# A decoder block's opening rearranged: norm, query projection, copy jobs and the first q block on other engines and in another order

## The reference

```python
xn = (x - mu) * rsqrt(var + 1e-05) * ln_gamma + ln_beta
q = (xn @ Wq.T + bq); k = (xn @ Wk.T + bk); v = (xn @ Wv.T + bv)
p = (pos_emb @ Wpos.T)
content_score = einsum('bthd,bshd->bhts', q + u_bias, k)
pos_score = rel_shift(einsum('bthd,phd->bhtp', q + v_bias, p))
attn = softmax((content_score + pos_score) / sqrt(dh))
x = layernorm(x + einsum('bhts,bshd->bthd', attn, v) @ Wout.T + bout)
...                                   # cross attention, layernorm
x = layernorm(x + moe(x))             # the last norm writes the output
```

## Time and profile before

| | |
|---|---|
| time, median of 3 runs (range) | 167.94 us (167.81 to 168.45) |
| the profiled execution: time, span | 167.27 us, 165.5 us |
| busy: PE, DVE, ACT, POOL | 142.8 (86%), 114.3 (69%), 100.9 (61%), 99.7 (60%) us |
| mean granted TensorE clock | 0.954 |

### The profile page before, as it was taken

One profiled execution on the slowest core, in us unless ns is written; L12 is line 12 of the kernel. 1 busy time (PEld: TensorE's weight loads), 2 busy tenths in 40 slices (PEclk: granted clock), 3 DMA queues, 4 the chain that ended last, 5 costly groups with the idle time before them and its releaser, 6 DMA issues.

```text
span 165.5 us, 5090 instructions
## 1 busy us (share of the span) xinstructions
PE 142.8 (86%) x2069; PEld 106.7 (64%) x2073; DVE 114.3 (69%) x331; ACT 100.9 (61%) x204; POOL 99.7 (60%) x125
## 2 busy tenths in 40 slices
PE   6739987999899999879898999599999979999920
PEld 2114436777689999767646767467779766766810
DVE  5610953989999998998636679952992899865150
ACT  3685753499698987389982451646665515665112
POOL 7669993047387677558978610606895605955642
PEclk9975999999999999999999999879999999999995
DMA  4560023320024550000004100000000000000001
GB/s 154 159 260 0 0 49 82 84 49 4 6 67 98 155 118 6 4 0 4 6 0 118 60 4 0 0 0 0 2 4 0 0 0 6 32 32 0 0 0 63
DMA packets 5593, 6.72 MB, mean 41 GB/s; under 512 B 1051, under 2 KB 4739, under 8 KB 5443
## 3 DMA queue, kind: packets, MB, share of 16 engines
q1 hardware_dynamic: 4995, 5.88, 12.5%
q10 hardware_dynamic: 576, 0.53, 1.0%
HBM read 3.79 MB, written 0.52 MB: 26 GB/s over the span
## 4 chain that ended last, share of the span: by engine, by line
PE 51%; DVE 14%; ACT 13%; POOL 12%; issue 4%; DMA 3%; SPq 1%; ACTq 0%; POOLq 0%; DVEq 0%
PE ps L849 49%; POOL pl L433 4%; ACT moe_c L545 4%; POOL rstd L392 3%; ACT ph L549 3%; POOL off L396 2%; DMA x_sb<-in_x 2%; PE ps L949 2%; DVE pm L696 2%; ACT q_c L493 1%; DMA qd<-q_dn 1%; SPq L361 1%; POOL ve L389 1%; DVE xh L733 1%; DVE st L639 1%
## 5 line engine op out<-in xcount | busy, mean ns | idle before, releaser
L433 POOL TENSOR_TENSOR pl<-moe_c,ph 128x1024 f16<-128x1024 f32 x16 | 34.0, 2133 | 20.0 <-ACT ph L549 20.0
L442 POOL TENSOR_TENSOR ph<-ph 128x512 f32<-128x512 f32 x16 | 20.6, 1291 | 21.1 <-PE ps L849 10.4
L849 PE MATMUL ps<-qd,kp 128*128 128x32 f16 (+1 forms) x768 | 24.7, 193 | 1.9 <-DMA qd<-q_dn 1.3
L849 PEld LDWEIGHTS ps<-qd,kp 128*128 128x128 f16 x768 | 23.6, 98 | 4.2 <-ACT q_dn L519 1.8
L696 DVE TRANSPOSE_TENSOR_REDUCE pm<-ps 128x32 f32<-128x1024 f32 x16 | 20.0, 1249 | 5.0 <-PE ps L849 4.4
L849 PE MATMUL ps<-moe_c,ph 128*128 128x128 f32 x144 | 19.6, 282 | 0.2 <-POOL ph L442 0.2
L849 PEld LDWEIGHTS ps<-moe_c,ph 128*128 128x128 f32 x144 | 17.4, 191 | 2.7 <-issue 2.4
L545 ACT ACTIVATE moe_c<-ps 128x1024 f32<-128x1024 f32 x16 | 16.5, 1032 | 1.6 <-PE ps L849 1.5
L849 PE MATMUL ps<-x2l,wfh 128*128 128x512 f32 x36 | 16.2, 449 | 0.4 <-DVE ph L768 0.4
L549 ACT ACTIVATE ph<-ps 128x1024 f16<-128x1024 f32 x16 | 16.4, 1028 | 0.0
L607 ACT ACTIVATE ph<-ps 128x512 f32<-128x512 f32 x18 | 10.8, 598 | 8.9 <-PE ps L849 8.5
(11 more groups left out here) (131 smaller groups left out, 279.9 us busy)
## 6 DMA issues: line engine op xcount, KB each, us to landing
qd<-q_dn SPq DMA_DIRECT2D x32, 64.0 KB, 2.1
ph<-in_w_ffn SPq DMA_DIRECT2D x1, 1152.0 KB, 5.1
moe_c<-in_w_down SPq DMA_DIRECT2D x1, 576.0 KB, 4.8
x_sb<-in_x SPq DMA_DIRECT2D x2, 256.0 KB, 3.4
out<-pl SPq DMA_DIRECT2D x4, 128.0 KB, 1.8
wp<-in_w_proj ACTq DMA_DIRECT2D x1, 320.0 KB, 4.5
kp_c<-in_ctx_t SPq DMA_DIRECT2D x1, 308.0 KB
cn<-in_ctx_n SPq DMA_DIRECT2D x1, 308.0 KB
```

What stands on the lines that cost most here:

```text
L433: nc.gpsimd.tensor_tensor(lo, p32[:, u % 2, :].rearrange("p (n i) -> p n i", i=CI), hi, ALU.subtract).then_inc(p_lo, 1)
L442: nc.gpsimd.tensor_tensor(hh[:, k % 3, :], gu[:, k % 3, :], cwr[:, k % 3, :], ALU.mult).then_inc(hid_ready, 1)
L849: return nc.tensor.matmul(o, w, r, start=start, stop=stop, skip_group_check=True)
```

## The change

- **Norm.** The first norm's scaling moves from ACT to DVE (`scaled`: subtract the mean, multiply by rstd, one instruction a tile). GpSimd makes no off for these four quarters, nor for the last two of the output norm.
- **PE's opening.** 16 warm-ups instead of 12, and one more in two places. The position product comes behind quarter 0, with the transpose of the bias row; the bias product behind quarter 1; the q product behind quarter 2. Quarter 3's `xnT` is written by DVE.
- **Jobs.** The order is queries, keys and tables of groups 0 and 1, over six banks; DVE copies out four of them (3, 5, 7, 9), ACT the others. A query job waits only for its own bias's rest.
- **Unit 0's q block.** GpSimd copies it, strip by strip, behind `wfh`; SP's first four DMAs carry only unit 1's half.
- **Order.** shift0 comes before scores2; GpSimd adds the bias between units 2 and 3; constants are set ahead of the passes; `qd` slot 1 is zeroed later.
- **End.** The last two quarters are scaled by DVE (`final2`, `final3`).

```diff
+JOBS = ([("query", 0, g, s) for s in (0, 1) for g in (0, 1)]
+        + [("key", e, g, 0) for e in (0, 1) for g in (0, 1)]
+        + [("table", 0, 0, 0), ("table", 0, 1, 0)]
         + [("query", 0, g, s) for g in (2, 3) for s in (0, 1)]
...
+JOBS_DVE = [3, 5, 7, 9]
+FIRST_BANKS = (0, 1, 2, 6, 7, 5, 0, 1, 2, 5)
...
-            job10 job11 scores0 job12 job13 scores1 job14 job15 scores2 job16 job17 shift0 shift1 query1 scores3
+            job10 job11 scores0 job12 job13 scores1 job14 job15 shift0 scores2 job16 job17 shift1 query1 scores3
...
-            y2 y3""")
+            y2 y3 final2 final3""")
...
+                    u0 = 1 if pair == 0 else 0
+                    sp.dma_start(qd[rows_h, slot, h, u0:2].rearrange("p c g s t -> p c (g s t)"),
...
+                if n < Q or n >= 4 * Q - 2:
+                    return
                 pool.wait_ge(rstd_ready, n + 1)
...
             pool.wait_ge(wf_in, 16)
             nc.gpsimd.tensor_copy(wfh[:, :, :], wf).then_inc(wf_hi, 1)
+            pool.wait_ge(qd_zero, PAIR_SLOTS)
+            wait_jobs(pool, 3)
             pool.wait_ge(wf_hi, 1)
+            for h in range(HG):
+                rows_h = slice(32 * h, 32 * h + 32)
+                if h:
+                    pool.wait_ge(q_first, h)
+                nc.gpsimd.tensor_copy(qd[rows_h, 0, h, 0].rearrange("p g s t -> p (g s t)"),
+                                      q_dn[rows_h, 0, 0, 0:GL].rearrange("p g s t -> p (g s t)")).then_inc(q_first, 1)
+            pool.wait_ge(q_first, HG)
             nc.gpsimd.tensor_tensor(wfl[:, :, :], wf, wfh[:, :, :].bitcast(F32), ALU.subtract).then_inc(wf_lo, 1)
...
+                elif stage == "bias":
+                    pool.wait_ge(xh_ready, Q)
+                    pool.wait_ge(bias_ready, 1)
+                    nc.gpsimd.tensor_tensor(x_sb[:, :, :], x_sb[:, :, :], rw[:, 1:2, :].broadcast_to([P, B, D]),
+                                            ALU.add).then_inc(xb_ready, 1)
...
-                if q == 1:
+                if q == 0:
                     act.wait_ge(p_ps, 1)
                     split_hi(kp_c[:, 0, B * T:KPT], ps[:, 2, 0:POS]).then_inc(kp_hi, 1)
+                    act.wait_ge(bvT_ps, 1)
+                    nc.scalar.copy(bvT[:, :], ps[:, 3, 0:P]).then_inc(bvT_ready, 1)
...
+            def scaled(n, q, dst, src, ready):
+
+                dve.wait_ge(rstd_ready, n + 1)
+                for b in range(q * QN, (q + 1) * QN):
+                    last = nc.vector.tensor_scalar(dst[:, b, :], src[:, b, :], mv[:, b, 0:1], rstd[:, b:b + 1],
+                                                   ALU.subtract, ALU.mult)
+                last.then_inc(ready, 1)
...
+            stats(x_sb, 2)
+            scaled(0, 0, xh, x_sb, xh_ready)
+            stats(x_sb, 3)
+            scaled(1, 1, xh, x_sb, xh_ready)
...
+            dve.wait_ge(xT_ps, Q)
+            nc.vector.tensor_scalar(xnT_i[:, GN:2 * GN, 1, :], ps[:, 4, 0:QN * T].rearrange("p (b i) -> p b i", i=TI),
+                                    cl[:, 4:5], cl[:, 5:6], ALU.mult, ALU.add).then_inc(xnT_last, 1)
...
+                elif stage == "final":
+                    scaled(norm_no("y", n), n, o_sb, z, o_last)
...
+            warm_up(16)
...
+                if q == 2:
                     pe.wait_ge(xnT_ready, 2)
                     mm(ps[:, 5, :], wp[:, 0, :], xnT_i[:, :, 0, :], True, True).then_inc(q_ps, 1)
...
-                elif 4 <= n < FIRST_JOBS:
-                    wait_job(pe, n - 4)
+                elif n >= 6:
+                    wait_job(pe, (0, 1, 2, 5, 3, 4)[n - 6])
...
-                    pe.wait_ge(q_lo, 2 * part + 2)
+                    pe.wait_ge(q_lo, 2 * part + s + 1)
...
                     if n == 0:
+                        wait_jobs(pe, FIRST_JOBS - 2)
+                        pe.wait_ge(q_first, HG)
+                    if n == 1:
+                        pe.wait_ge(q_in[0], 16 * HG)
+                    if n == 2:
                         wait_jobs(pe, FIRST_JOBS - 1)
```

More of the change, by code:

```diff
@@ L495, in norm @@
                 last.then_inc(ready, 1)
[L497 to L500, removed]
+            for q in range(Q - 1):
                 act.wait_ge(xT_ps, q + 1)
@@ L525, in _ @@
                 split_hi(kp_c[:, 0, g * GT:(g + 1) * GT], ps[:, (3, 4)[g], :], cl[:, 1:2]).then_inc(kp_hi, 1)
[L526 to L529, removed]
+            for n in JOBS_ACT:
+                if n < FIRST_JOBS:
+                    copy_out(n)
             def value_heads(g):
@@ L650, in _ @@
                 nc.vector.tensor_tensor(qb[:, s:s + 1], cl[:, 0:1], cl[:, 2 + s:3 + s], ALU.add).then_inc(qb_ready, 1)
+            scaled(2, 2, xh, x_sb, xh_ready)
+            scaled(3, 3, xh, x_sb, xh_ready)
             dve.wait_ge(kp_hi, 1)
@@ L655, in _ @@
                                     ALU.subtract).then_inc(kp_lo, 1)
+            dve.wait_ge(rw_in, 16)
+            dve.wait_ge(bias_ps, 1)
+            nc.vector.tensor_tensor(rw[:, 1, :], ps[:, 3, P:P + D], rw[:, 1, :], ALU.add).then_inc(bias_ready, 1)
+            dve.wait_ge(xT_ps, Q)
+            nc.vector.tensor_scalar(xnT_i[:, GN:2 * GN, 1, :], ps[:, 4, 0:QN * T].rearrange("p (b i) -> p b i", i=TI),
+                                    cl[:, 4:5], cl[:, 5:6], ALU.mult, ALU.add).then_inc(xnT_last, 1)
             def q_rests(ih):
@@ L674, in copy_out @@
                 nc.vector.tensor_copy(dst, src).then_inc(rep_dve, 1)
-            for n in JOBS_DVE[:FIRST_JOBS // 2]:
+            for n in JOBS_DVE:
                 copy_out(n)
-            dve.wait_ge(rw_in, 16)
-            dve.wait_ge(bias_ps, 1)
-            nc.vector.tensor_tensor(rw[:, 1, :], ps[:, 7, 0:D], rw[:, 1, :], ALU.add).then_inc(bias_ready, 1)
             def value_rest(g):
@@ L852, in _, with warm_up @@
             pe.wait_ge(warm_set, 1)
-            for n in range(12):
-                mm(ps[:, 6, :], i_warm[:, 0:P], i_warm[:, :], True, True)
+            def warm_up(n):
+                for _ in range(n):
+                    mm(ps[:, 6, :], i_warm[:, 0:P], i_warm[:, :], True, True)
+            warm_up(16)
             pe.wait_ge(id_in, 16)
@@ L864, in _ @@
                     mm(ps[:, 2, 0:POS], wp[:, 2, :], pe_sb[:, :], True, True).then_inc(p_ps, 1)
-                if q == 3:
+                    pe.wait_ge(rw_in, 16)
+                    nc.tensor.transpose(ps[:, 3, 0:P], rw[:, 0, :], ident[:, :]).then_inc(bvT_ps, 1)
+                    warm_up(1)
+                if q == 1:
+                    pe.wait_ge(bvT_ready, 1)
+                    mm(ps[:, 3, P:P + D], bvT[:, :], wp[:, 4, :], True, True).then_inc(bias_ps, 1)
+                    warm_up(1)
+                if q == 2:
                     pe.wait_ge(xnT_ready, 2)
                     mm(ps[:, 5, :], wp[:, 0, :], xnT_i[:, :, 0, :], True, True).then_inc(q_ps, 1)
-            for g in range(G):
-                pe.wait_ge(xnT_ready, 3 + g)
-                mm(ps[:, (3, 4)[g], :], wp[:, 1, :], xnT[:, g * GT:(g + 1) * GT], True, True).then_inc(k_ps, 1)
+            pe.wait_ge(xnT_ready, 3)
+            pe.wait_ge(bias_ready, 1)
+            mm(ps[:, 3, :], wp[:, 1, :], xnT[:, 0:GT], True, True).then_inc(k_ps, 1)
+            pe.wait_ge(xnT_last, 1)
+            mm(ps[:, 4, :], wp[:, 1, :], xnT[:, GT:2 * GT], True, True).then_inc(k_ps, 1)
             def copy_job(n):
@@ L903, in _ @@
                 copy_job(n)
[L904 to L907, removed]
             def value(g):
@@ L1034, in _ @@
                         wait_jobs(pe, SECOND_JOBS - 1)
-                    if n % 2 == 0:
+                    if n % 2 == 0 and n:
                         pe.wait_ge(q_in[n // 2 % PAIR_SLOTS], 16 * HG * (n // 2 // PAIR_SLOTS + 1))
```

50 lines of the change are left out of this document (23 added, 27 removed).

## The result

The changed kernel takes 157.58 us (median of 4 runs, 157.46 to 157.81) against 167.88 us for the kernel before beside it (165.89 to 168.45): a ratio of 0.9426 (95% interval 0.9344 to 0.9507). The profiled execution took 157.81 us with a span of 156.0, 9.46 less than the one before; the working had 8.15.

The account below looks back on a forecast made before the run. Bound by the opening chain before the first scores, then DVE's 2.99 us pitch, then the end chain. 167.27 − 6.7 + 0.15 − 1.6 = 159.1 us profiled; median 0.67 above, 159.8, range 157.8 to 163.0.

Parts of the forecast that it names:

- the working: Whole kernel: opening lead 6.7, order cost 0.15, end gain 1.6, so 8.15 us off the profiled execution, to 159.1.
- Mechanism: Opening to end: first scores come 6.7 us earlier, units move forward as a block, the end shortens by 1.6.
- Norm: Opening: GpSimd passes fall from 1.71 to 1.1 us; DVE scales each quarter in 0.43, by about 6.5 to 9.7.
- Warm-ups: PE's opening: four more cost 0.9 to 1.8 us; PE free at 7.4 to 8.4, taken as 7.7, setting the transposes.
- Strips: Unit 0's q block: four GpSimd copies of 0.6 us, 2.75 in all; data at 18.9, scores0 at 19.0.
- Order: shift0 before scores2: the second q projection comes some 0.15 us later on PE, cost 0.15.
- End: Last outputs: y3's rstd at 161.15, DVE scales two batches by 161.65, gain 1.6 us.
- half-clock stretch at 106: Late units: the stretch may vanish when all before it moves; 1.6 us allowed, in the range only.
- The clock did not fall in the opening: Rival, opening: clock stays low or falls, lead only 3.0, time 163.5 us; chance 0.10.
- two-input: Rival, unit 0's q block: GpSimd copies take 4.6 us for 2.75, time 161.7, or 162.5 with clock loss; chance 0.09.
- strided rate: Rival, unit 0's q block: copies at 2.57 us each, scores0 at 26.9, no change or slower; chance 0.07.
- DVE held by GpSimd: Rival, norm and end: a scaled quarter waits up to 0.71 us for a power, time 161.1; chance 0.08.

Follow-up runs that it names:

- 3: The changed kernel with unit 0's q block written by SP's four DMAs again instead of GpSimd; 158.74 us, ratio 0.9532.
- 6: The changed kernel with the first norm as before, GpSimd making off and ACT scaling; 159.41 us, ratio 0.962.
- 8: The changed kernel with the old job order (tables, queries, keys), its DVE copies and two PE waits; 158.48 us, ratio 0.9544.
- 2: The kernel before with PE kept busy: 13 warm-ups and 4 more ahead of each later quarter's transposes; 164.71 us, ratio 0.9898.
- 12: Kernel 4 with two warm-ups instead of twelve; 159.41 us, ratio 0.9535.
- 1: The kernel before with only the end changed: DVE scales the last two quarters, no off for them; 165.0 us, ratio 0.9922.
- the control: The changed kernel itself, unchanged, timed again; 158.39 us (157.53 to 159.5), ratio 0.9527.
- 11: Kernel 4 with GpSimd's four strip copies issued without waiting for one another; 157.72 us, ratio 0.9421.
- 7: The changed kernel with shift0 behind job 17 again, after scores2, as before; 157.38 us, ratio 0.9469.
- Kernel 4: The changed kernel with 12 warm-up products and without the two single ones; 156.56 us, ratio 0.94.
- kernel 10: Kernel 4 with ten short products of 8 columns behind the warm-ups; 157.02 us, ratio 0.9395.
- 9: Kernel 4 once more, unchanged, as control; 156.84 us (156.63 to 158.06), ratio 0.9391.

## Why the prediction was right, and where it was too small

**Mechanism.** Opening brought forward, units moved as a block, a shorter end: all three are in the trace, and the experiments price the parts: strips on GpSimd 1.3 (3), norm on DVE 1.6 to 2.5 (6), order of jobs 1.07 (8), the clock 1.3 to 1.4 (2, 12), the end 1.37 (1). Each part was taken out or put in alone, so they need not add up to the lead; that the q product comes ahead of quarter 3's transposes, and that DVE writes quarter 3's `xnT`, was not tried by itself.

**Norm.** Passes of 1.0 us (4.59 to 7.56 for three) for 1.1, quarters scaled by 6.29, 7.45, 8.22 and 9.21 for 6.5, 7.6, 8.5 and 9.7. A pair of tensor_scalar of 128 columns took 0.57 to 0.60 and not 0.43; one of them, partly beside the other, took 0.31 to 0.35. The row of 512 columns (0.426) bounded one above, but halving it was wrong: by estimate from these rows, 384 columns fewer save only about 0.1. It cost nothing, as the warm-ups covered the first quarter.

**Warm-ups.** This is the mis-sized term. Sixteen ended at 6.82, where 7.4 to 8.4 was forecast. The working took 0.44 for each of the first twelve and 0.9 to 1.8 for the other four. In the trace the products start 0.43 apart up to the ninth, at 4.83, and the last seven, from 5.15, 0.22 apart: the rise of the clock came that early. That gives the transposes at 6.66 for 7.7, the q product's end at 9.97 for 11.15, and, carried through unchanged (DVE's copy at 14.96 for 16.15, strips ready at 17.80 for 18.9), a lead of 7.75 for 6.7. In the control the same sixteen ended at 7.7, as forecast, and the scores came at 18.83, 0.17 ahead of the forecast of 19.0. So the term is not one number: between two executions of one program it moved by 0.9 us, and the 1.05 by which the first beat the working was luck; the control's median, 158.39, lies inside the range. The Trainium skill, "TensorE: Matmul & The Clock Gate", Part 1 (the HAM clock gate), says so much: the count of slow products at a kernel's start differs from run to run. These runs agree, with products 0.43 apart up to 4.83 in the one and up to 6.53 in the other.

**Strips.** 2.61 for 2.75. Between two strips lie 0.06 for the 0.09 assumed, with the waits and without (11).

**Order.** 0.15 forecast; 0.32 (4.93 against 4.61) in this execution, 0.05 in the control, and nothing gained by undoing it (7).

**End.** 1.38 for 1.6: a pair of scalings takes 0.60 for the 0.43 assumed, and the last ve of GpSimd 0.32 for 0.22.

**What was not in the sum.** The stop of PE in unit 12 costs 0.9 here (3.60 against 2.70), and the half-clock stretch at 106 that did not come gives back 1.5 (lead from 6.59 to 8.09). The second was named in the range, with 1.6 allowed, but not in the likeliest sum. The difference of 1.31 in the profiled executions is +1.05 (warm-ups), −0.17 (order), −0.22 (end), −0.85 (the stop's 0.9 and hundredths in other units) and +1.5 (stretch). The two large gains are the clock's, and no run shows that the change made either: such a stretch came in the changed kernel's control too (5). The gap of medians, 10.3, is wider still because the profiled execution before was 0.6 below its median and the one after 0.2 above its own.

**Rivals.** The clock did not fall in the opening; experiment 12 shows what a late rise would cost, 1.3 at the scores. Strips at the two-input or the strided rate: 0.65 a strip rules out both. DVE held by GpSimd: the scaled pairs took 0.57 to 0.60 whether GpSimd's power ran beside them (5.72, the power from 5.88) or GpSimd was idle (153.17), so no wait for a power is in them. By the Trainium skill, "SBUF — State Buffer", section on who interferes with whom, such a tensor_scalar can wait for a whole instruction of GpSimd; this trace does not show it. The one sign of it is small: at the end GpSimd's ve beside DVE's scaling took 0.32, where without it it takes 0.22.

**A faster version.** Kernel 4 is at 156.56 and 156.84 us, the changed kernel at 157.58 and 158.39: about 1 us, on different chips, with ranges that overlap only in their tails (to 158.06, from 157.46) and ratios whose intervals overlap. At a mean granted clock of 0.986 and above, kernel 4's nine executions took 156.48 to 157.38 and the changed kernel's five 157.46 to 157.81. In the two first traces the stop in unit 12, absent in kernel 4, is 0.9 of a difference of 1.28. That the stop is the cause of the gain is not shown, as kernel 10 has the stop in its trace and a median of 157.02, with its four executions at that clock at 156.41 to 157.14.

## What to carry to other kernels

Follow an opening as one chain through all engines and put each step's start into the sum: a step that only sets when the next begins, such as warm-ups, counts too (here its end moved the scores by 0.9 us between two executions). Before believing a difference of 1 us, look for stretches at 1.2 GHz in the profile of both: here they came and went between executions and cost 0.9 and 1.5 us; compare times at like mean granted clocks, where two medians can hide an edit's 1 us (8) or feign one (5). And count instructions as well as microseconds: in the traces, ten short products, or six fewer, moved a stop of PE into or out of a place where it mattered.

## What the runs showed that I had not expected

PE's stops without a visible wait come behind a fixed number of its products, whatever the time: 1102 in six executions (the changed kernel, its control, experiments 6 to 8 and 10), and, by 0.17, in experiment 1; 974 and, by 0.18 in the weight loads, 1102 in the one with two warm-ups; 974, by 0.16 in the weight loads, and 1229, by 0.27, in the changed kernel; and 1229 in experiments 3 and 6. They are 128 apart, to within a missing record. Each product is a weight load and a multiplication, so 256 instructions; the page's instruction queue moved 0.26 MB in 16 packets, 16 KB each, which would be 64 bytes an instruction. That suggests that PE waits for its next instructions there.

The packets' own records in the traces bear this out. One 16 KB packet comes for every 128 products. Windows of the changed kernel (the two last figures are DMA and GB/s), 16 GB/s for 1 us, then nothing up to the end of the stop:

```profile
54.90:55.90 1.00, 1.00 (x45) 1.00 (x42) 0.93 (x3) 0.79 (x1) 0.32 (x2) 1.00 0.06 16
55.90:57.15 1.25, 0.80 (x33) 0.70 (x28) 1.24 (x5) 0.00 (x0) 1.25 (x1) 1.00 0.00 0
```

The packet landed at 55.88 and PE went on at 57.16, 1.28 later. In experiment 10 it landed at 54.92 and PE went on at 56.35; in the one with two warm-ups 53.96 and 55.49; every stop named above ends 1.2 to 1.5 us behind such a landing. It also shows why PE passes some of these places: in experiments 3, 4, 9 and 11 the packet had landed 1.25 to 1.85 us before PE came to the place behind 1102 products. In the seven traces that stop behind 1102 first named, that packet had begun 1.4 to 1.8 us after the 974th product; in experiments 3, 4, 9 and 11 it began 0.35 to 1.3 us after it. Why it begins at different times no run shows; that PE waits for the packet is read from these times, as the profile names no releaser.

The warm-ups show the clock where the granted clock of the windows does not: that column reads 1.00 from the start, while the products come 0.43 us apart and later 0.22. With two warm-ups the column reads 1.00 from 7 to 11, and a pair of transposes takes 0.66, as it took 0.69 in the kernel before at a granted 0.50, and 0.38 behind it. So the start level is read from the products' spacing, not from the column.
